# Heads 1 to 7 of a graph attention layer: source tile 3 also in three rounded passes, its low part built by two transfers

## The reference, cut to what matters

```python
h = (x @ W.T).reshape(n, heads, out_ch)
a_src = einsum('nhc,hc->nh', h, att_src); a_dst = einsum('nhc,hc->nh', h, att_dst)
e = leaky_relu(a_src[src] + a_dst[dst], 0.2)
m = segment_max(e, dst); ex = exp(e - m[dst]); denom = segment_sum(ex, dst)
alpha = ex / (denom[dst] + EPS)
out = segment_sum(alpha[:, :, None] * h[src], dst)
```

## Time and profile before

| | before |
|---|---|
| median of 3 runs | 715.13 us (715.05 to 715.64) |
| the profiled execution's own time | 716.03 us |
| its span, first to last instruction | 714.2 us |
| PE / DVE / ACT / POOL busy over the span | 98% / 74% / 59% / 15% |
| mean granted TensorE clock | 1.000 |

### The profile page before, as it was taken

How to read it: one execution, slowest core, us unless ns; L and a number is a source line. 1 busy time by engine, 2 the same in 40 slices (tenths; PEclk the granted TensorE clock), 3 DMA queues, 4 the chain that set the end, 5 groups by cost and what they waited for, 6 DMA issues and landing times.

```text
span 714.2 us, 13401 instructions
## 1 busy us (share of the span) xinstructions
PE 702.2 (98%) x4670; PEld 658.0 (92%) x4670; DVE 529.2 (74%) x878; ACT 420.0 (59%) x862; POOL 106.9 (15%) x95
## 2 busy tenths in 40 slices
PE   8899999999999999999999999999999999999997
PEld 7699999878899999999999999999999999999997
DVE  5899888698899999999999674445568752737232
ACT  4665584288688888888888755444443333522202
POOL 2558121000000000000000000000123331222202
PEclk9999999999999999999999999999999999999999
DMA  8627666649311112303230343201882734315102
GB/s 283 215 70 198 201 182 174 175 137 317 113 73 37 72 37 73 101 17 97 66 146 0 96 114 70 65 2 35 246 281 51 218 86 194 100 57 176 44 23 67
DMA packets 50226, 84.10 MB, mean 118 GB/s; under 512 B 14633, under 2 KB 35951, under 8 KB 49280
## 3 DMA queue, kind: packets, MB, share of 16 engines
q1 hardware_dynamic: 44492, 65.69, 30.7%
q10 hardware_dynamic: 4500, 13.82, 5.9%
q0 software_dynamic: 1184, 3.92, 1.9%
HBM read 68.09 MB, written 15.33 MB: 117 GB/s over the span
## 4 chain that ended last, share of the span: by engine, by line
PE 89%; DMA 4%; DVE 3%; ACT 2%; issue 1%; ACTq 0%; POOL 0%; SPq 0%; DVEq 0%
PE bank L1392 21%; PE bank L1537 13%; PE bank L1464 12%; PE bank L1368 12%; PE bank L1267 10%; PE bank L1641 4%; DMA w1n_sb<-in_W 3%; PE bank L1613 3%; PE bank L1182 3%; PE bank L1518 2%; PE bank L1667 1%; DVE x2f L2278 1%; PE bank L1184 1%; ACT L L884 1%; ACT PT L902 1%; PE bank L1197 1%
## 5 line engine op out<-in xcount | busy, mean ns | idle before, releaser
L1392 PE MATMUL bank<-PT,h1s 125*128 125x250 f32 x730 | 161.0, 374 | 0.0
L1392 PEld LDWEIGHTS bank<-PT,h1s 125*128 125x128 f32 x730 | 135.3, 190 | 14.4
L2044 DVE SCALAR_TENSOR_TENSOR L<-asb,nadh 125x1250 f32<-125x1250 f32 x80 | 117.9, 1516 | 4.5 <-PE bank L1368 3.5
L2053 DVE CUSTOM_DVE_ANT_0 L<-L,LC 125x1250 f32<-125x1250 f32 x80 | 113.5, 1456 | 0.2
L902 ACT COPY PT<-bank 125x500 f32<-125x500 f32 x165 | 87.4, 607 | 36.9 <-PE bank L1368 36.9
L884 ACT ACTIVATE L<-L,nm 125x1250 f32<-125x1250 f32 x80 | 108.2, 1380 | 1.5 <-DVE nm L2053 1.4
L1368 PE MATMUL bank<-ident,L 125*125 125x125 f32 x800 | 94.2, 273 | 1.6 <-ACT PT L902 1.1
L1368 PEld LDWEIGHTS bank<-ident,L 125*125 125x125 f32 x800 | 90.9, 189 | 3.3 <-issue 3.2
L1850 DVE TENSOR_TENSOR hotr<-iota,r 125x1500 f16<-125x1500 f16 x50 | 46.5, 931 | 8.1 <-PE bank L1184 4.5
L1537 PE MATMUL bank<-h_hi,PT_hi 125*125 125x384 f32 x200 | 41.5, 350 | 0.0
L1537 PE MATMUL bank<-h_lo,PT_hi 125*125 125x384 f32 x200 | 40.5, 342 | 0.0
(11 more groups left out here) (284 smaller groups left out, 1347.0 us busy)
## 6 DMA issues: line engine op xcount, KB each, us to landing
asb<-src_logit_rows SPq DMA_DIRECT2D x7, 1250.0 KB, 5.9
atom_w<-in_atom_inT SPq DMA_DIRECT2D x5, 1152.0 KB, 11.9
atom_w<-in_atom_outT SPq DMA_DIRECT2D x5, 1152.0 KB, 9.1
log_count_scratch<-LCw SPq DMA_DIRECT2D x10, 546.9 KB
LC<-log_count_scratch SPq DMA_DIRECT2D x10, 546.9 KB
LCt<-log_count_scratch SPq DMA_DIRECT2D x10, 546.9 KB
h_scratch<-h1st ACTq DMA_DIRECT2D x10, 448.0 KB
rdT<-reciprocal_scratch SPq DMA_DIRECT2D x8, 500.0 KB, 4.9
```

Of the source, the lines that this page charges most:

```text
L1392: mm = pe.matmul(sums, h1s[q][:, s, :], PT[p][:, s, :], start=(s == 0), stop=(plain and s == NT - 1))
L2044: dve.scalar_tensor_tensor(L[r][:, :], asb[q][0:NP, 1, :], nadh[q][:, t:t + 1], asb[q][0:NP, 0, :], ALU.add, ALU.max).then_inc(stt_done, 1)
L2053: dve.tensor_tensor_reduce(out=L[r][:, :], in0=L[r][:, :], in1=LC[:, t, :], scale=-1.0, scalar=-FLOOR, op0=ALU.add, op1=ALU.min, accum_out ...
```

## The change

In heads 1 to 7 source tile 3 also leaves the fp32 matmuls. ACT rounds both tiles of bank 1 with one instruction (PT_hi is now 2 x 250 wide) and writes tile 3 negated as fp32 into PT[p][:, 3, :]. POOL then issues, for each of the 35 groups, a plain transfer of that negated tile into PT_neg, and, when it has landed, a transfer that adds PT_hi of tile 3 to PT_neg. PT_neg is then PT_hi - P, the low part with its sign turned. PE multiplies it with h1p_neg, the negated features. POOL doesn't wait for the adding transfer before it starts on the next group. PE waits for it (lower_moved) ahead of the last matmul of the group. For room, rrow shrinks to one row set, so that ACT waits for the store of the batch before (rden_stored), and wrow2 moves. Two semaphores of the second layer are merged into tb_full and tb_evac, with the same waits.

```diff
+            def lower_by_sum(hh, kk):
+                n, p = 2 * NG * hh + kk, kk % 2
+                pool.wait_ge(tb_evac, NG * n + (PART // 2 + 1))
+                alone(pool)
+                pool.dma_start(PT_neg[p][:, :].bitcast(F32), PT[p][:, PART + 1, :]).then_inc(raw_moved, 16)
+                pool.wait_ge(raw_moved, 16 * n + (16 - 16 * NG))
+                alone(pool)
+                pool.dma_start(PT_neg[p][:, :].bitcast(F32), PT_hi[p][:, 1, :].bitcast(F32), accum_op=ALU.add
+                               ).then_inc(lower_moved[p], 16)
+            for kk in range(NG, 2 * NG):
+                lower_by_sum(0, kk)
+            with pool.Fori(1, H // 2) as hh:
+                for kk in range(2 * NG):
+                    lower_by_sum(hh, kk)
...
# ACT, evac, bank 1 of heads 1 to 7
-                        act.copy(PT_hi[(k - lag) % 2][:, :], turned[0:NP, 0:GW])
-                        act.copy(PT[(k - lag) % 2][:, PART + 1, :], turned[0:NP, GW:2 * GW]).then_inc(tb_evac, 1)
+                        act.copy(PT_hi[(k - lag) % 2][:, :, :],
+                                 turned[0:NP, 0:2 * GW].rearrange("p (s n) -> p s n", s=2))
+                        act.activation(PT[(k - lag) % 2][:, PART + 1, :], turned[0:NP, GW:2 * GW], ACT.Copy, scale=-1.0
+                                       ).then_inc(tb_evac, 1)
...
# ACT, part_higher, once for each head
-                act.copy(h1p[q][:, 0, :], h1s[q][:, PART, :]).then_inc(features_high, 1)
+                act.activation(h1p_neg[q][:, :], h1s[q][:, PART + 1, :], ACT.Copy, scale=-1.0)
+                act.copy(h1p_hi[q][:, :, :], h1s[q][:, PART:PART + 2, :]).then_inc(features_high, 1)
...
# ACT, rows_out_of
-                to = rlast[:, ds(hh if k else hh + -1, 1), 0:NP] if (t0, t1) == (LATE, NT) else None
-                if to is None:
-                    to = rrow[t0:t1, ds(h, 1), 0:NP]
-                act.copy(to.rearrange("t a n -> t (a n)"), bank[4][0:t1 - t0, 0:NP]).then_inc(rden_rows, 1)
+                freed(act, rden_stored, 16 * m)
+                act.copy(rrow[0:t1 - t0, 0:NP], bank[4][0:t1 - t0, 0:NP]).then_inc(rden_rows, 1)
...
# PE, aggregate
-                    if plain or s != PART:
+                    if plain or s not in (PART, PART + 1):
...
-                    pe.matmul(sums, h1p[q][:, 0, :], PT_hi[p][:, :], start=False, stop=False)
-                    pe.matmul(sums, h1p[q][:, 1, :], PT_hi[p][:, :], start=False, stop=False)
-                    mm = pe.matmul(sums, h1p[q][:, 0, :], PT_lo[p][:, :], start=False, stop=True)
+                    for s in range(2):
+                        pe.matmul(sums, h1p_hi[q][:, s, :], PT_hi[p][:, s, :], start=False, stop=False)
+                        pe.matmul(sums, h1p_lo[q][:, s, :], PT_hi[p][:, s, :], start=False, stop=False)
+                    pe.matmul(sums, h1p_hi[q][:, 0, :], PT_lo[p][:, :], start=False, stop=False)
+                    pe.wait_ge(lower_moved[p], 16 * NG * hh + 16 * ((k - lag) // 2 - (NG // 2 - p)))
+                    mm = pe.matmul(sums, h1p_neg[q][:, :], PT_neg[p][:, :], start=False, stop=True)
...
# DVE, lower_part, once for each head
-                    dve.tensor_tensor(h1p[q][:, 1, :], h1s[q][:, PART, :], h1p[q][:, 0, :].bitcast(F32), ALU.subtract
-                                      ).then_inc(features_lower, 1)
+                    dve.tensor_tensor(h1p_lo[q][:, :, :], h1s[q][:, PART:PART + 2, :], h1p_hi[q][:, :, :].bitcast(F32),
+                                      ALU.subtract).then_inc(features_lower, 1)
```

More of the change, by code:

```diff
@@ L63 @@
 BATCHES = 3 * H // 2
+TURNED_BANKS = NG * NG * H
 PART = 2
@@ L290, in gnn_ffn_kernel @@
         h1s = [sb(f"h1s{q}", [NP, NT, C], F32, p3) for q in range(2)]
-        rrow = sb("rrow", [NT, H, NP + 3], F32, p3)
-        rlast = sb("rlast", [NT - LATE, H // 2, NP + 3], F32, p3)
-        wrow2 = sb("wrow2", [2, HC], F32, p3)
+        rrow = sb("rrow", [NT, NP + 3], F32, p3)
         rdA = [sb(f"rdA{p}", [C, H, NP], F32, p3) for p in range(2)]
-        h1p = [sb(f"h1p{q}", [NP, 2, C], F32R, p3) for q in range(2)]
-        PT_hi = [sb(f"PT_hi{p}", [NP, GW], F32R, p3) for p in range(2)]
+        h1p_hi = [sb(f"h1p_hi{q}", [NP, 2, C], F32R, p3) for q in range(2)]
+        h1p_lo = [sb(f"h1p_lo{q}", [NP, 2, C], F32R, p3) for q in range(2)]
+        h1p_neg = [sb(f"h1p_neg{q}", [NP, C], F32R, p3) for q in range(2)]
+        PT_hi = [sb(f"PT_hi{p}", [NP, 2, GW], F32R, p3) for p in range(2)]
         PT_lo = [sb(f"PT_lo{p}", [NP, GW], F32R, p3) for p in range(2)]
-        pad3 = sb("pad3", [128, 4064 - 2 * H * NP - 512 - 1512 - 16], F32, p3)
+        PT_neg = [sb(f"PT_neg{p}", [NP, GW], F32R, p3) for p in range(2)]
+        pad3 = sb("pad3", [128, 640], F32, p3)
         PT = [sb(f"PT{s}", [NP, NT, GW], F32, p3) for s in range(2)]
+        once = ExitStack()
+        sb("pad_hT", [C, (H - 1) * N], F32, once)
+        wrow2 = sb("wrow2", [2, HC], F32, once)
+        once.close()
         hT = sb("hT", [C, H, N], F32, p3)
@@ L396, in gnn_ffn_kernel @@
         row_full, row_out = sem("row_full"), sem("row_out")
-        lct_in, bo_in, t5_high = sem("lct_in"), sem("bo_in"), sem("t5_high")
+        lct_in, bo_in = sem("lct_in"), sem("bo_in")
         slope5 = sem("slope5")
-        t5_full, t5_evac, y_full, y_evac = sem("t5_full"), sem("t5_evac"), sem("y_full"), sem("y_evac")
+        t5_evac, y_full, y_evac = sem("t5_evac"), sem("y_full"), sem("y_evac")
         x5_in, xb_done = sem("x5_in"), sem("xb_done")
@@ L416, in gnn_ffn_kernel @@
         w1_hi_done, w1_lo_done, xT_lo_done = sem("w1_hi_done"), sem("w1_lo_done"), sem("xT_lo_done")
+        raw_moved, lower_moved = sem("raw_moved"), [sem(f"lower_moved{p}") for p in range(2)]
         features_high, features_lower, lower_done = sem("features_high"), sem("features_lower"), sem("lower_done")
@@ L506, in _, with store_reciprocals @@
                 load_w2n(k)
-            def store_reciprocals(m, h, rows, t0, t1):
+            def store_reciprocals(m, h, t0, t1):
                 sp.wait_ge(rden_rows, m + 1)
                 sp.dma_start(rden_d[ds(h, 1), t0 * NP:t1 * NP].rearrange("a (t n) -> (a t) n", t=t1 - t0),
-                             rows.rearrange("t a n -> t (a n)")).then_inc(rden_stored, 16)
+                             rrow[0:t1 - t0, 0:NP]).then_inc(rden_stored, 16)
             def store_even(hh):
-                store_reciprocals(3 * hh, 2 * hh, rrow[:, ds(2 * hh, 1), 0:NP], 0, NT)
+                store_reciprocals(3 * hh, 2 * hh, 0, NT)
             def store_odd_first(hh):
-                store_reciprocals(3 * hh + 1, 2 * hh + 1, rrow[0:LATE, ds(2 * hh + 1, 1), 0:NP], 0, LATE)
+                store_reciprocals(3 * hh + 1, 2 * hh + 1, 0, LATE)
             def store_odd_last(hh):
-                store_reciprocals(3 * hh + 2, 2 * hh + 1, rlast[:, ds(hh, 1), 0:NP], LATE, NT)
+                store_reciprocals(3 * hh + 2, 2 * hh + 1, LATE, NT)
             with sp.Fori(0, H // 2 - 1) as hh:
@@ L1013, in slope_5 @@
                 if i > 0:
-                    act.wait_ge(t5_full, 5 * i)
+                    act.wait_ge(tb_full, TURNED_BANKS + 5 * i)
                 else:
@@ L1027, in evac_5 @@
                 for b in range(5):
-                    act.wait_ge(t5_full, 5 * i + b + 1)
+                    act.wait_ge(tb_full, TURNED_BANKS + 5 * i + b + 1)
                     if b == 0 and not first:
@@ L1031, in evac_5 @@
                     act.copy(PT5_hi[:, 2 * b:2 * b + 2, :],
-                             bank[T5BANK[i][b]][0:NP, 0:2 * GW].rearrange("p (s n) -> p s n", s=2)).then_inc(t5_high, 1)
+                             bank[T5BANK[i][b]][0:NP, 0:2 * GW].rearrange("p (s n) -> p s n", s=2)).then_inc(tb_evac, 1)
             def ffn_5(i, tokens=False):
@@ L1519, in turn_5 @@
                                           L5[j][:, (2 * b + s) * NP:(2 * b + s + 1) * NP], ident[0:NP, 0:NP])
-                mm.then_inc(t5_full, 1)
+                mm.then_inc(tb_full, 1)
             def turn_units(part):
@@ L1535, in add_5 @@
                     if j == 0 and b == 0 and s % 2 == 0 and term != "hl":
-                        pe.wait_ge(t5_high if term == "hh" else t5_evac, 5 * i + s // 2 + 1)
+                        if term == "hh":
+                            pe.wait_ge(tb_evac, TURNED_BANKS + 5 * i + s // 2 + 1)
+                        else:
+                            pe.wait_ge(t5_evac, 5 * i + s // 2 + 1)
                     mm = pe.matmul(bank[2 + 2 * j + b][0:NP, 0:HALF], rows[:, s, j * NP:(j + 1) * NP],
@@ L2070, in lower_part @@
                 dve.tensor_tensor(PT_lo[p][:, :], bank[turned_bank(first, k - lag, PART // 2)][0:NP, 0:GW],
-                                  PT_hi[p][:, :].bitcast(F32), ALU.subtract).then_inc(lower_done, 1)
+                                  PT_hi[p][:, 0, :].bitcast(F32), ALU.subtract).then_inc(lower_done, 1)
             def step(hh, k, **at_end):
@@ L2175, in lower_5 @@
                 for b in range(5):
```

(2 more changed lines are left out.)

## The result

The changed kernel takes 721.58 us (median of 4 runs, 719.82 to 722.65), the kernel before 715.38 in the same series. The ratio is 1.0076, 95% interval 1.0063 to 1.009: slower by 0.8%, outside the range of 712.3 to 717.5. The profiled execution took 722.65 us for a span of 720.8.

The account below looks back on a forecast made before the run. PE was taken as the bound, with DVE and ACT close behind. Saving 2.45 us on PE and losing 0.35 at the hand-over made -2.1 us, from 715.13 to 713.0 us; range 712.3 to 717.5.

Parts of the forecast that it names:

- The arithmetic: PE's sums in 35 groups: one fp32 tile replaced by three rounded passes, 0.07 us saved each, 2.45 us in all.
- ACT's 0.2 us a step: ACT's wider cast and scaled copy of bank 1: 0.21 to 0.23 us more each step, ahead of the exponentials.
- The 0.35 us for the hand-over: Where the stage meets the second layer: ACT 0.21 us later and PE's 0.14 us gain lost, 0.35 us in all.
- The quiet pair: POOL's two transfers without other traffic: landings of 2.8 and 3.5 us plus 0.3 for releases, 6.6 us.
- the loaded pair: POOL's two transfers beside the second layer's weights: 10.4 us scaled by bytes, 0.1 over budget, taken as nothing.
- The unscaled reading of the same row: Both transfers beside the weights at 6.3 us each plus releases: 12.9 us, 2.6 over budget, once; kept for the range.
- The second rival: POOL's pairs late only in loaded stretches, 125 rows perhaps on fewer DMA engines: 715 to 721 us; chance 0.17.
- the budget: Time for POOL's two transfers, from ACT's release of the tile to PE's last pass: 10.3 us.
- The third rival: POOL's pair late in every group, PE stalling ahead of the last pass: 748 us at 12.3 us a pair; chance 0.10.
- the fourth: DVE's instructions hold up POOL's issues, up to 1.47 us each: 729 us; chance 0.04.
- A tie of engines: ACT's spare of 0.0 to 0.1 us vanishes, so the step gets no shorter: 714 to 715.2 us; chance 0.13.

Follow-up runs that it names:

- without the transfers: Changed kernel with PT_neg set to zero once instead of POOL's 70 transfers, all six rounded passes kept: 713.66 us, ratio 0.9966 to the kernel before.
- transfers in two pieces: Changed kernel with each of POOL's transfers cut into 112 and 13 rows: 727.84 us, ratio 1.0158 to the kernel before.
- reciprocals later: Changed kernel with the reciprocals of tiles 2 and 3 loaded only after the last adding transfer landed: 719.2 us, ratio 1.0061 to the kernel before.

## Why the prediction was wrong

The arithmetic was right. -2.45 + 0.35 = -2.1 us was forecast, and without the transfers the kernel gave -2.3 (medians) and -2.34 (stage). ACT's 0.2 us a step fitted, with 0.61 us of idle time left where 0.6 was said. The 0.35 us for the hand-over was too much: without transfers PE waits 0.4 us for ACT's cast, where it waited 0.32 before. The quiet pair came out right as a sum: 0.58 us from ACT's tile to the issue (301.10 to 301.68), 2.7 between the issues, 3.0 for the adding one, 6.3 us against 6.6. In part this is luck. Both landings were put too high (2.8 and 3.5, measured 2.1 and 3.0), and the two releases too low (0.3, measured 1.2).

**The step that failed is the loaded pair**, "Scaled by bytes (2.8 us extra for 336 KB, 1.0 for 125 KB) it is 6.6 + 1.0 + 2.8 = 10.4 us. I take 0.1, so nothing". It was 14.4 us. For the plain transfer I scaled the delay that 336 KB had suffered down to 122 KB, as if a small transfer were delayed in proportion. The runs show that it isn't: the plain 122 KB landed in 7.8 us beside the weights, 5.7 us more than alone. The unscaled reading of the same row, 6.3 us each, gave 12.9 us and 2.6 us of stall, and was kept for the range. That was still too little: the landings were 7.8 and 5.4, and the releases 1.2.

The second rival, late in loaded stretches only, is what happened, though not by the few engines that it supposed. It gave 2.6 to 4 us for the weights (4.0 measured) and 0.3 to 1 us for each of seven heads. Only five loads of logits fall in the stage, and three of them cost 0.2 to 0.3 us. Its own sum is wrong. 2.6 to 4 and seven times 0.3 to 1 make 4.7 to 11 us, so 717.7 to 724 us, and not "+2 to +8" and 715 to 721. With the right sum the measured 721.6 lies in this rival, and all of it lies outside the range of 712.3 to 717.5, which so left out chances of 0.31 and not "just under 0.2".

Two terms were missing altogether. One is the end of the stage: rdA and rdT are loaded with 1000 KB each beside the last two groups, and the budget of the last group is 9.0 us and not 10.3. POOL works its transfers off in order and handed 0.6 us of group 38's lateness to group 39, and the adding transfer beside rdT lost 3.5 us. The stall was 2.3 us, and with rdT loaded later it went. The other is the clock, 1.7 us behind the long stall. Together with the weights they are 8.0 us. The high end of the range, 717.5, held 2.6 us for the weights' stall but neither of these, which is why 721.6 lies outside.

The third rival (every pair late) and the fourth (DVE holding up POOL) are out: the issues keep their length beside DVE's instructions, 0.55 and 0.84 us, and 30 of 35 groups never waited. A tie of engines is out by the run without transfers.

On the loaded landing: the weights took 14.2 us to land, and the pair beside them was done only when they were. The Trainium skill ("DMA: Bandwidth & Descriptors", "Queues, rings and completion order") says that each DMA engine takes turns between the queues by whole packets of several descriptors. The trace shows 2.7 us instead of 0.7 from the plain transfer's first packet to its last, which fits with turns. It also shows 3.3 us more before the first packet. Whether that is a wait for turns, or for something ahead of the queues, no run here separates.

## What to carry to other kernels

When work is handed to a chain of small transfers with a deadline, go through every bulk load of that stage, the one-off ones too, and ask what the chain takes beside each. A transfer of 122 KB that lands in 2.1 us alone took 7.8 us just behind loads of 0.6 and 3 MB, far more than its size suggests, and a queue that works in order passes its lateness on. Look at the last group by itself: its deadline can be shorter than that of the others. Here cutting and spacing the loads, which was worth nothing in the kernel before, turned a loss of 0.8% into a gain of 0.26%.

## What the runs showed of the hardware that was not expected

An adding transfer costs only a little more than a plain one of the same 122 KB: 0.84 against 0.55 us to issue, 3.0 against 2.1 us to land in quiet. POOL issues 0.58 us after ACT's instruction ends. A plain transfer of 125 rows ran on all 16 DMA engines. PE's granted clock fell for part of the next 8 us after stalls of 4.0 us (changed kernel), and 3.9 and 2.5 us (transfers in two pieces, 0.57 in the 4 us from 370 and 0.66 in those from 410). After one of 3.0 us (reciprocals later) it did not. So the length of the stall alone doesn't tell.
